# Local attention on 32 units with overlapping key tiles in place of 48, with the mask work shared out anew between TensorE, VectorE and GpSimd

## What is computed

```python
q = split_heads(x @ wq, H); k = split_heads(x @ wk, KVH); v = split_heads(x @ wv, KVH)
q, k = (rope(q, BASE_L), rope(k, BASE_L)); q, k = (qk_norm(q), qk_norm(k))
k, v = (repeat_kv(k), repeat_kv(v))
diff = i[:, None] - i[None, :]
mask = (diff >= 0) & (diff < WIN)            # WIN = 32
return merge_heads(sdpa(q, k, v, mask)) @ wo
```

## Time and profile before

| | us |
|---|---|
| median of 3 runs | 1262.74 (1262.25 to 1264.91) |
| the profiled execution: its time | 1263.66 |
| the profiled execution: its span | 1261.9 |
| TensorE busy, whole span | 1141.8 (90%) |
| VectorE busy | 987.2 (78%) |
| ScalarE busy | 830.2 (66%) |
| GpSimd busy | 444.9 (35%) |

### The profile page before, as it was taken

One profiled execution on the slowest core, in us unless ns is written; L12 is line 12 of the kernel. 1 busy time (PEld: TensorE's weight loads), 2 busy tenths in 40 slices (PEclk: granted clock), 3 DMA queues, 4 the chain that ended last, 5 costly groups with the idle time before them and its releaser, 6 DMA issues.

```text
span 1261.9 us, 36707 instructions
## 1 busy us (share of the span) xinstructions
PE 1141.8 (90%) x15602; PEld 693.7 (55%) x15602; DVE 987.2 (78%) x1556; ACT 830.2 (66%) x1229; POOL 444.9 (35%) x582
## 2 busy tenths in 40 slices
PE   4488889898989999778999999999999999999985
PEld 3133434344435655455666666676666666666662
DVE  7869685877768888896887887788778877887755
ACT  3498898989887867545556655665666566656541
POOL 2203221211206448855533433333333333333310
PEclk8599999999999989998999999999999999999997
DMA  3114120020213331100210110111111111111102
GB/s 106 34 25 137 50 91 35 18 101 18 69 51 135 119 134 69 50 18 20 82 24 22 30 30 16 26 30 24 24 27 23 28 23 27 28 23 28 27 6 67
DMA packets 37329, 59.78 MB, mean 47 GB/s; under 512 B 6416, under 2 KB 12464, under 8 KB 37168
## 3 DMA queue, kind: packets, MB, share of 16 engines
q1 hardware_dynamic: 35760, 56.61, 15.3%
q10 hardware_dynamic: 1408, 0.84, 0.3%
HBM read 22.58 MB, written 16.78 MB: 31 GB/s over the span
## 4 chain that ended last, share of the span: by engine, by line
PE 51%; DVE 4%; ACT 2%; issue 1%; DVEq 0%; ACTq 0%
PE psum L1327 9%; PE psum L1463 7%; PE psum L1416 6%; PE psum L1438 5%; PE psum L1402 5%; PE psum L1337 4%; PE psum L1347 4%; PE psum L1489 3%; PE psum L1424 2%; PE psum L1387 2%; PE psum L1359 2%; ACT ffn_probs L1646 2%; PE psum L1393 1%; PE psum L1367 1%; PE psum L1455 1%
## 5 line engine op out<-in xcount | busy, mean ns | idle before, releaser
L818 ACT ACTIVATE att_probs<-psum 128x1024 f32<-128x1024 f32 (+2 forms) x384 | 350.7, 988 | 44.5 <-PE psum L673 44.3
L1757 POOL TENSOR_TENSOR ffn_rot<-ffn_rot,ffn_rot_sin 128x512 f32<-128x512 f32 x128 | 160.2, 1273 | 372.5 <-DVE ffn_rot L1788 372.5
L717 PE MATMUL psum<-att_probs,att_v 128*32 128x256 f32 (+3 forms) x3712 | 201.4, 343 | 6.5 <-DVE att_probs L1010 3.2
L673 PE MATMUL psum<-att_q_stack,att_k_parts 64*128 64x512 bf16 (+4 forms) x1280 | 142.1, 296 | 41.8 <-ACT att_probs L818 30.4
L717 PEld LDWEIGHTS psum<-att_probs,att_v 128*32 128x32 f32 x3712 | 96.1, 110 | 72.0 <-issue 41.8
L1010 DVE TENSOR_TENSOR att_probs<-att_probs,att_causal_mask 128x1024 f32<-128x1024 f32 (+1 forms) x80 | 95.9, 1214 | 35.3 <-ACT att_probs L818 35.2
L673 PEld LDWEIGHTS psum<-att_q_stack,att_k_parts 64*128 64x128 bf16 x1280 | 43.5, 94 | 144.5 <-ACT att_probs L818 104.0
L1639 ACT ACTIVATE ffn_max_t<-psum 68x128 bf16<-68x128 bf16 x64 | 17.5, 273 | 156.8 <-PE psum L1375 156.7
L1646 ACT ACTIVATE ffn_probs<-psum 128x1024 f32<-128x1024 f32 x64 | 65.6, 1025 | 59.1 <-PE psum L1402 59.1
L1608 ACT ACTIVATE ffn_sq<-psum 128x512 f32<-128x512 f32 x128 | 74.7, 595 | 22.0 <-PE psum L1327 21.1
L604 POOL TENSOR_TENSOR att_rot<-att_qk 128x1280 f32<-128x1280 f32 x6 | 16.5, 2756 | 204.9 <-ACT att_qk L849 204.9
(11 more groups left out here) (222 smaller groups left out, 2443.1 us busy)
## 6 DMA issues: line engine op xcount, KB each, us to landing
ffn_v_back<-ffn_v SPq DMA_DIRECT2D x120, 130.0 KB, 2.4
att_q_stack<-q_rows SPq DMA_DIRECT2D x28, 512.0 KB, 3.6
q_rows<-att_q_high SPq DMA_DIRECT2D x21, 256.0 KB, 4.5
q_rows<-att_q_mid SPq DMA_DIRECT2D x21, 256.0 KB, 4.2
q_rows<-att_q_low SPq DMA_DIRECT2D x14, 256.0 KB, 4.0
xres<-in_hidden SPq DMA_DIRECT2D x4, 512.0 KB, 6.1
out<-ffn_qk_t SPq DMA_DIRECT2D x3, 512.0 KB, 3.2
tail_f_wqkv<-in_f_wqkv SPq DMA_DIRECT2D x1, 768.0 KB, 4.5
```

Of the source, the lines that this page charges most:

```text
L673: ins = T.matmul(psum[:, banks[i] + at:banks[i] + at + width], k_parts[rows, p % 3, j, kt * P:(kt + 1) * P], q_stack[rows, turn % 2, j, q0 ...
L717: ins = T.matmul(psum[32 * g:32 * g + V_PAD, (4 + cc) * BANK + lo - cc * BANK: (4 + cc) * BANK + hi - cc * BANK], v[:, p % 4, kt, g, shift ...
L818: act.activation(probs[:, n % E_BUFS, 2 * j:2 * j + 2, 0:width], ps2((step % 2) * 2).rearrange("p (h c) -> p h c", h=2)[:, :, 0:width], AC ...
L1757: steps.did(pool.tensor_tensor(out, out, halves(k.rot_sin[:, n % 2, :])[:, :, 1 - half, :], ALU.add), g["added"] if half else None)
```

## The change

The local block gets eleven key tiles that overlap, each starting 96 keys after the last (`LOCAL_KEYS`: 0, 96, ..., 864, 896). A tile then takes only those queries whose 32 keys all lie in it and that no tile before has taken: 128, then nine times 96, then 32. That is 1024 columns a turn, in two units of exactly 512: tiles 0 to 4 and 5 to 10. Phases 4 to 7 so have 32 units (144 to 175) in place of 48.

- TensorE adds its mask in step `j = 0` only, for head 0. VectorE multiplies heads 1 and 2 in one instruction of 1024 elements, GpSimd head 3 in one of 512.
- Seven of the eleven tiles do not start at a multiple of 128, so their values lie in two of the old tiles. Six DMAs a local phase (`shift_values`) copy them into `att_v_moved` (two buffers); `v` itself is packed at 32 columns a head in place of 48.
- The spread of local phase `p` is issued ahead of another turn's gather: of turn `4p - 3` for phases 4 to 6, of turn `4p - 1` for phase 7. `shift_values(p)` stands ahead of the gather of turn `4p - 1`.
- The tables place the side work on 16 ticks fewer. The QKV steps of phase 7 take 11 ticks in place of 20 (152 to 163; before 153 to 173), and those of phase 6 start at the same tick but end at 152 and not 156: its rotation's `cos`, `head_reduce`, `sin` and `add` move from ticks 144 to 149 to ticks 139 to 143, ahead of the first local unit. The last ticks are 180 and 197.

```diff
+NEW_KEYS = P - WINDOW_A
+LOCAL_KEYS = tuple(range(0, S - P, NEW_KEYS)) + (S - P,)
+MOVED = [i for i, key in enumerate(LOCAL_KEYS) if key % P]
...
-LOCAL_UNITS = ((0, 1, 2), (3, 4, 5), (6, 7))
-OPENS = ((0, 6), (0, 3))
-CLOSES = ((2, 5), (3, 7))
+LOCAL_UNITS = ((0, 1, 2, 3, 4), (5, 6, 7, 8, 9, 10))
+OPENS = ((0, 6), (0, 5))
+CLOSES = ((2, 5), (4, 10))
+SPREAD_TURNS = {GROUP * p - (0 if p < len(PHASES) // 2 else 1 if p == len(PHASES) - 1 else 3): p
+                for p in range(1, len(PHASES))}
+SHIFT_TURNS = {GROUP * p - 1: p for p in range(len(PHASES) // 2, len(PHASES))}
...
-QKV_AT = (-12, 2, 32, 53, 82, 101, 126, 153)
+QKV_AT = (-12, 2, 32, 53, 82, 101, 126, 152)
...
-POST_AT = (176, 185)
+POST_AT = (166, 172)
...
                 for kts in LOCAL_UNITS:
-                    out.append((p, r, [(kt, kt * P, min(SPAN_A, S - kt * P), i * SPAN_A, kt // 4)
-                                       for i, kt in enumerate(kts)]))
+                    pieces, at = [], 0
+                    for kt in kts:
+                        q0, q1 = (LOCAL_KEYS[i - 1] + P if i else 0 for i in (kt, kt + 1))
+                        pieces.append((kt, q0, q1 - q0, at, q0 // CHUNK))
+                        at += q1 - q0
+                    out.append((p, r, pieces))
...
-    DVE_HEAD, POOL_HEAD = 1, 3
+    DVE_HEADS, POOL_HEAD = slice(1, 3), 3
...
+            def shift_values(p):
+
+                sp.wait_ge(v_ready, 2 * (p + 1))
+                if p - 2 >= len(PHASES) // 2:
+                    sp.wait_ge(pv_done, last_unit[GROUP * (p - 1) - 1] + 1)
+                tiles = lambda buf, count: buf[:, 0:count * V_TILE].rearrange("p (t c) -> p t c", t=count)
+                src, dst = tiles(v[:, p % 4], TILES), tiles(v_moved[:, p % 2], len(MOVED))
+                for i in range(PARTS):
+                    t0, off = divmod(LOCAL_KEYS[MOVED[i]], P)
+                    count = len(MOVED[i::PARTS])
+                    sp.dma_start(dst[0:P - off, i::PARTS],
+                                 src[off:P, t0:t0 + 3 * count - 2:3]).then_inc(v_shifted, 16)
+                    sp.dma_start(dst[P - off:P, i::PARTS],
+                                 src[0:off, t0 + 1:t0 + 3 * count - 1:3]).then_inc(v_shifted, 16)
...
-                if a == 1:
+                if a == 1 and j == 0:
 
                     T.matmul(psum[:, banks[0]:banks[0] + width_of(pieces)], keep.ident_bf[:],
-                             keep.local_bf[:, 0:width_of(pieces)], start=True, stop=True, skip_group_check=True)
+                             local_seen(keep.local_bf, n), start=True, stop=True, skip_group_check=True)
...
                     if n == first_unit[turn] and r == 0:
                         pe.wait_ge(v_ready, 2 * (p + 1))
+                        if a == 1:
+                            pe.wait_ge(v_shifted, 16 * 2 * PARTS * (p + 1 - len(PHASES) // 2))
...
                     if phase_of(n) == 1:
-                        rows = local_row(n, DVE_HEAD)
-                        c.did(V.tensor_tensor(rows, rows, keep.local_mask[:, 0:width_of(UNITS[n][2])], ALU.mult), masked)
+                        rows = probs[:, n % E_BUFS, DVE_HEADS, :]
+                        seen = local_seen(keep.local_mask, n).rearrange("p (o c) -> p o c", o=1)
+                        c.did(V.tensor_tensor(rows, rows, widen(seen, list(rows.shape)), ALU.mult), masked)
```

116 lines of the change are left out of this document (71 added, 45 removed).

## The result

The changed kernel is slower: 1269.58 us (median of 4 runs, 1267.43 to 1271.79) against 1262.72 for the kernel before, run beside it (1262.25 to 1264.91). The ratio is 1.0049, 95% interval 1.0030 to 1.0069. Forecast were 1253.4 us, a range of 1238 to 1270, and "faster" with a chance of 0.62. The median lies just inside the range, at its upper end; the sign is wrong.

A forecast was written before the change was run, and what follows sets the result against it. VectorE was to become the fullest engine in local units paced mostly by TensorE: 10.3 us saved there, 1.0 charged for moved steps, so -9.3 us and 1253.4 us as time of runs, range 1238 to 1270.

The forecast's parts named there:

- TensorE, part by part: Local units: a unit takes 1.98 or 2.06 us, and TensorE's busy time falls by 30.6 to 91.2 us.
- VectorE's masks: Local units: a two-head mask takes 1.61 us, 32 of them 51.5 us, in place of 43.8 now.
- the 112.2 of the sum: VectorE's need in the local units: 113.3 - 43.8 - 8.8 + 51.5 = 112.2 us, making it the fullest engine.
- I give it 7 us of idle time, less than half of today's: VectorE in the local units: 7 us idle, bounds none or 16.2, so the units take 119.2 us, 10.3 less.
- The third rival: Phase 7's steps, one tick apart across engines, pace the stream and TensorE pauses: 1282 us, slower; chance 0.21.
- The forecast's own 1246 to 1260: Range of the main case, from the bounds of VectorE's idle time and mask; chance 0.52.
- The moved steps: VectorE's phase 6 steps, 8.8 us, moved ahead of unit 144: charged 1 us, between 0 and 3.
- The last division, output product and addition stand as far behind the last unit as before: The close behind the local units: its distance from the last unit was to stay unchanged.
- GpSimd's total: GpSimd's masks over the local units: 65.1 us become 32 x 1.61 = 51.5, so it has room.
- the prediction's own sign: Test for being wrong: time outside the local units changes by more than 3 us, or a dense TensorE unit exceeds 2.3.
- The spread of phase 7: SyncE's copies of values before the gather of turn 27: charged 0, at most 5 us.
- first rival: VectorE's and GpSimd's masks never run side by side, so their joint time binds: gain 1.6 us, 1261 us; chance 0.17.

The follow-up runs named there:

- e7_mix3: Changed kernel, but in 19 units with long VectorE side steps TensorE masks heads 0 to 2 and VectorE none: 1253.93 us, ratio 0.9934 to before.
- e8_mix3_end: e7_mix3 with GpSimd masking nothing in the last three units (TensorE takes head 3) and phase 4's second transposes one tick earlier: 1252.80 us, ratio 0.9922.
- e4_one_head: Changed kernel with VectorE's second head given back to TensorE, so VectorE masks head 1 alone: 1260.92 us, ratio 0.9979 to the kernel before.

## Why the prediction was wrong

**TensorE, part by part: right.** 1.92 us against 1.98 for a dense unit with 40 value instructions. The 48 of the other unit took 1.02 us from their start to the next product (507.94 to 508.96), 21 ns each, under the 1.10 that I took. Its busy time in the local stretch was 88.7 us as recorded against 91.2, and some 98 with the missing mask products, but part of that at the lower clock.

**VectorE's masks: right.** 1.59 us against 1.61, and 50.8 us for 32 against 51.5. Its load, 109.0 us of the local stretch, was even below the 112.2 of the sum.

**"I give it 7 us of idle time, less than half of today's": the step that failed.** VectorE was idle 20.5 of the 129.0 us (108.5 busy), so more than before and beyond the upper bound of 16.2 that I gave. The local units so took 129.0 us and not 119.2. The argument went by the average over 129 us. But the steps of phases 6 and 7 and of the close lie in three stretches, where VectorE lacked time and was as full as TensorE before the change, and its free time lies in two others, 13.3 of the 20.5 us, where TensorE and the exponentials set the pace. Masks can lag by three units at most, so free time in one stretch doesn't serve the next. A sum by stretches comes nearer but is not whole. The fullest engine of each stretch of the changed kernel (VectorE 80.4 us, TensorE 34.5 by the estimate above, GpSimd 7.4 behind 505 us) adds up to some 122 us of the 129.0; in the other 7 no engine is full.

**The third rival, and what was wrong in it.** It had the sign, the place and the look of the profile: TensorE waiting for rotations and divisions, at the lower clock behind each pause. It put the cause on one-tick distances, and that was not it: with slack but the same masks nothing was gained (1.0043), and with the changed kernel's tables, one step moved, but no masks in these stretches the waits vanished (0.9878). It also looked at units 153 to 163 alone. Of the six long waits only two were there. Two came at the end of phase 6, of which I had priced only the steps moved ahead of unit 144, and two in the close.

**The range.** That the median lies inside it is no merit of the forecast: it reached 1270 only to take in half of the third rival. The forecast's own 1246 to 1260 was also narrower than the bounds it names: an idle time of 16.2 gives 1262.6, a mask of 2.0 us 1265.9.

**The moved steps: nearly right.** The first local mask came at 383.6, as before, where I charged 1 us.

**"The last division, output product and addition stand as far behind the last unit as before": wrong, 5.8 us.** With 16 ticks fewer, GpSimd's gate and shift (12.5 us in the changed kernel) stand ahead of its last three masks, and TensorE waited 4.00 us for them. I counted GpSimd's total and found room. Relieving the last three units of GpSimd moved the first FFN product 4.0 us earlier (e7_mix3 to e8_mix3_end, where one tick of phase 4 moved too), though the run's time by only 0.1%. By the prediction's own sign, over 3 us outside the local units, it was wrong here.

**The spread of phase 7: charged 0, "at most 5".** In the changed kernel the gather behind it cost 0.7 us, and TensorE's other waits hid the rest: it cost 6.26 when phase 7 came one tick later, and 2.40 to 3.09 once VectorE was relieved.

**The joint time of the two masks (first rival).** The mechanism is real and stronger than I had it. The Trainium skill ("SBUF — State Buffer", section "SBUF: two separate sides") says that such a VectorE instruction and a GpSimd one hold a common port in turn, each for its whole length. The one-element instruction of 0.18 us that took 1.22 agrees. But the two engines were not full together: 108.5 and 75.0 us in 129.0. It acted through the length of VectorE's work in the full stretches, and leaving GpSimd's masks out gave 14 us. That took 34.0 us of masks from GpSimd and 7.8 from VectorE and gained 1.2 points; e4_one_head took 15.3 from VectorE and gained 0.7. How much of VectorE's lack of time is its own work, and how much is standing behind GpSimd, was not separated.

**Open.** The part behind the first product of the FFN, in which no line was changed, took 738.8 us before, 737.6 in the changed kernel, and 737.2 to 741.8 in the versions. It ate 3 of the 5.6 us that e4_one_head had gained by then. What sets it was not tried. How much of the loss was the lower clock and how much the pauses themselves was not separated either.
